# The front of a decoder's first stage put into one block

## The reference, cut to what matters

```python
xn1 = layernorm(x)                                   # outer norm, no weights
mu, var = mean(xn1), var(xn1)
xn = (xn1 - mu) * rsqrt(var + 1e-5) * norm_w + norm_b
xc, z = split(xn @ W_in)                             # 256 -> 2 x 512
xc = silu(conv4(xc) + conv_b)                        # causal, 4 taps
dbc = xc @ x_proj_w                                  # 512 -> 1 + 16 + 16
dt = softplus(dbc[:, :1] * dt_w + dt_b)
B, C = dbc[:, 1:17], dbc[:, 17:]
h = exp(dt * A) * h + dt * B * xc                    # over the tokens, 16 states
y = (h . C + xc * D) * silu(z)
x = x + (y @ W_out + xn1)
```

## Time and profile before

| | us |
|---|---|
| median of 3 runs | 2512.63 |
| lowest and highest | 2509.29, 2513.92 |
| the profiled execution | 2509.35 |
| its span, first to last instruction | 2507.6 |

### The profile page before, as it was taken

The page is one execution under the profiler, slowest core; times in us unless marked ns, Lnnn a source line. Parts: engine busy times, 40 slices in busy tenths (PEclk is TensorE's granted clock), DMA queues, the critical chain, the costliest instruction groups (busy, mean ns, idle before and its releaser), DMA issues. The chain is left out here.

```text
span 2507.6 us, 37343 instructions
## 1 busy us (share of the span) xinstructions
PE 1985.6 (79%) x10490; PEld 1106.8 (44%) x10490; DVE 1682.1 (67%) x3093; ACT 989.2 (39%) x2104; POOL 826.8 (33%) x603
## 2 busy tenths in 40 slices
PE   5945555557799898776999999978887799974777
PEld 2412222223466666333333333355444455542777
DVE  5769999993777777485555555556432466667994
ACT  2654333330577776225565555511211111111321
POOL 1036666560422220001666666610000022211342
PEclk8979999998899999897999999989989799986888
DMA  1024444441766663200455545353011421126220
GB/s 62 1 91 146 146 133 150 143 133 48 147 135 138 140 140 90 94 30 18 145 164 174 170 142 165 91 184 96 0 32 27 128 93 59 68 90 220 86 81 30
DMA packets 137566, 264.96 MB, mean 106 GB/s; under 512 B 34630, under 2 KB 89831, under 8 KB 134936
## 3 DMA queue, kind: packets, MB, share of 16 engines
q1 hardware_dynamic: 119864, 220.96, 30.0%
q0 software_dynamic: 13824, 37.77, 4.8%
q10 hardware_dynamic: 3808, 5.38, 0.8%
HBM read 214.61 MB, written 49.44 MB: 105 GB/s over the span
## 5 line engine op out<-in xcount | busy, mean ns | idle before, releaser
L552 PE MATMUL mamba_y<-mamba_read,ident 128*128 128x448 f32 x512 | 228.8, 571 | 162.6 <-DVE mamba_read L524 162.6
L500 POOL TENSOR_TENSOR xn<-mamba_u,mamba_b_all 128x896 f32<-128x896 f32 x128 | 263.3, 2078 | 259.7 <-DMA mamba_b_all<-mamba_b 259.7
L517 DVE TENSOR_TENSOR_SCAN mamba_state<-mamba_state,xn 128x896 f32<-128x896 f32 x128 | 258.9, 2023 | 6.5 <-POOL xn L500 6.0
L2378 ACT ACTIVATE moe_w_tile<-moe_w 128x1216 f32 x144 | 175.1, 1217 | 146.1 <-PE moe_y_ps L2330 131.8
L552 PEld LDWEIGHTS mamba_y<-mamba_read,ident 128*128 128x128 f32 x512 | 87.8, 191 | 303.2 <-DVE mamba_read L524 254.2
L2315 PE MATMUL moe_up_ps<-moe_w_tile,moe_xT 128*64 128x352 f32 x1152 | 204.3, 476 | 1.3 <-issue 1.3
L2277 POOL DMA_INDIRECT moe_y<-moe_y_sb,moe_index x144 | 158.0, 1097 | 108.5 <-DVE moe_y_sb L2351 75.6
L963 DVE CUSTOM_DVE_ANT_0 xattn_sm<-xattn_s_ps,xattn_mask 112x375 f32<-112x375 f32 x256 | 138.7, 545 | 80.9 <-PE xattn_s_ps L856 71.3
L1054 ACT ACTIVATE xattn_prob<-xattn_sm,xattn_least 112x375 f32<-112x375 f32 x256 | 154.4, 604 | 74.7 <-DVE xattn_least L963 70.8
L2330 PE MATMUL moe_y_ps<-moe_w_tile,moe_hT 128*64 128x256 f32 (+1 forms) x1152 | 177.3, 403 | 0.0
L2271 POOL DMA_INDIRECT moe_xg<-moe_tok,moe_index x144 | 152.8, 1061 | 53.6 <-issue 37.5
(11 more groups left out here) (310 smaller groups left out, 3931.4 us busy)
## 6 DMA issues: line engine op xcount, KB each, us to landing
moe_w<-moe_w SPq DMA_DIRECT2D x64, 480.0 KB
mamba_b_all<-mamba_b SPq DMA_DIRECT2D x64, 448.0 KB, 3.5
mamba_c_all<-mamba_c SPq DMA_DIRECT2D x64, 448.0 KB, 4.7
soft_w<-soft_w SPq DMA_DIRECT2D x16, 1024.0 KB, 8.4
moe_f_part<-moe_y SPq DMA_DIRECT2D x14, 1024.0 KB, 5.7
soft_logits<-soft_logit SPq DMA_DIRECT2D x28, 512.0 KB, 2.6
soft_logit<-soft_logits SPq DMA_DIRECT2D x14, 1024.0 KB, 5.2
xattn_ks<-xattn_k_parts SPq DMA_DIRECT2D x32, 375.0 KB, 6.5
```

What stands on the lines that cost most here:

```text
L500: pool.tensor_tensor(fed[:, PAIR * s + c], u[:, c0 + c, tok], b_all[:, s], ALU.mult).then_inc(input_ready, 1)
L517: dve.tensor_tensor_scan(state[:, q % 2, 0:HW], state[:, q % 2, 0:HW], fed[:, q % RING], 0.0, ALU.mult, ALU.add).then_inc(state_ready, 1)
L552: mm = pe.matmul(y[:, q % PAIR, w, 0:CW], g.ident[:], read[:, q % 2, w * CW:(w + 1) * CW], start=False, stop=False, skip_group_check=True)
L2378: pipelined(act, SLOT_TILES, RING, [weight_placer(act, 0, lambda to, src: act.activation(to, src, ACT.Copy)), silu, copy_hidden])
```

## The change

All work of the first stage up to the scan stands in one block.

- x is loaded in four chunks, each with a semaphore of its own that is kept across the stages, and the first block no longer waits for x or the identity. The stage's weights are issued at the start of the new block, and `dt_rep` is not loaded any more.
- The mean and the variance v of x are computed once. The outer norm is (x - m) / sqrt(v + e), and the second norm of it (x - m) / sqrt(v (1 + e) + e * e) before its weights; ACT takes both roots of the same variance. DVE makes the product with the second, ACT applies weight and bias. The first's reciprocal `r1` is taken by DVE, spread by PE in four one-row matmuls, copied by ACT, and POOL multiplies and adds it to x chunk by chunk.
- dt's column is the 33rd of the same product as B and C; its row is copied to SBUF with them and spread over the partitions by a one-row matmul (`spread_raw`).
- In softplus ACT copies `raw` to SBUF, and POOL does the linear part and the relu as eight tensor_scalar of 448 columns a chunk, and the sum. Exp and Ln are taken from one table set that has both.
- DVE's order is convolve 0, 1, then feed 0, convolve 2, feed 1, convolve 3, feed 2, feed 3, where `feed(j)` is the product with `xs`. A's exponential moves from the start of the block to its end. The first half of B and C is stored as soon as it is there.

```diff
-            sp.dma_start(g.x[:], ins["xT"].rearrange("(h p) t -> p h t", p=P)).then_inc(loaded, 16)
-            sp.dma_start(g.ident[:], ins["ident"]).then_inc(loaded, 16)
-            sp.wait_ge(loaded, 32)
+            x_in = ins["xT"].rearrange("(h p) t -> p h t", p=P)
+            for j in range(NCH):
+                sp.dma_start(g.x[:, :, chunk(j, CW)], x_in[:, :, chunk(j, CW)]).then_inc(g.x_loaded[j], 16)
+            sp.dma_start(g.ident[:], ins["ident"]).then_inc(g.ident_loaded, 16)
...
-            norm(g, g.x, xn1, prefetch=prefetch)
-            norm(g, xn1, g.xn, norm_wb[:, 0], norm_wb[:, 1], beside=add_residual)
...
+                @block.gpsimd
+                def _(pool):
+                    def residual(i):
+                        pool.wait_ge(r1_copied, i + 1)
+                        for h in range(DH):
+                            pool.tensor_tensor(xm[:, i, h], xm[:, i, h], r1[:, i], ALU.mult).then_inc(res_scaled, 1)
+                        pool.wait_ge(res_scaled, DH * (i + 1))
+                        x = g.x[:, :, chunk(i, CW)]
+                        pool.tensor_tensor(x, x, xm[:, i], ALU.add).then_inc(res_done, 1)
+                    def soften(j):
+                        pool.wait_ge(raw_copied, j + 1)
+                        for c in range(DIC):
+                            pool.tensor_scalar(u[:, c, chunk(j, CW)], raw_sb[:, j % 2], dt_w[:, c:c + 1], dt_b[:, c:c + 1], ALU.mult, ALU.add).then_inc(lin_done, 1)
+                        for c in range(DIC):
+                            pool.wait_ge(lin_done, DIC * j + c + 1)
+                            pool.tensor_scalar(u[:, c, chunk(j, CW)], u[:, c, chunk(j, CW)], 0.0, None, ALU.max).then_inc(relu_done, 1)
+                        for c in range(DIC):
+                            pool.wait_ge(ln_done, DIC * j + c + 1)
+                            pool.wait_ge(relu_done, DIC * j + c + 1)
+                            pool.tensor_tensor(dt[:, c, chunk(j, CW)], dt[:, c, chunk(j, CW)], u[:, c, chunk(j, CW)], ALU.add).then_inc(dt_done, 1)
+                    pool.wait_ge(normed, NCH)
+                    for i in range(NCH):
+                        residual(i)
+                    for j in range(NCH):
+                        soften(j)
...
-                            mm = pe.matmul(raw[:, 0:CW], dt_rep[:, c], xs[:, c, chunk(j, CW)], start=(c == 0), stop=(c == DIC - 1))
...
+                    def spread_raw(j):
+                        pe.wait_ge(bc_copied, j + 1)
+                        wait(pe, raw_copied, j)
+                        wait(pe, abs_done, DIC * j)
+                        pe.matmul(raw[:, 0:CW], g.ones[RAW:RAW + 1], bc_sb[RAW:RAW + 1, chunk(j, CW)], start=True, stop=True, tile_position=(RAW, 0)).then_inc(raw_ready, 1)
...
+                    pe.wait_ge(std1_ready, 1)
+                    project_xc(0)
+                    pe.wait_ge(normed, NCH)
+                    pe.wait_ge(rstd1_ready, len(parts))
+                    spread_r1(0)
+                    spread_r1(1)
+                    project_z(0)
+                    spread_r1(2)
+                    spread_r1(3)
+                    pe.wait_ge(small_loaded, 48)
+                    pe.wait_ge(r1_copied, NCH)
+                    for j in range(1, NCH):
+                        project_xc(j)
+                        derive(j - 1)
+                        project_z(j)
+                        spread_raw(j - 1)
+                    derive(NCH - 1)
+                    spread_raw(NCH - 1)
...
+                    convolve(0)
+                    convolve(1)
+                    for j in range(2, NCH):
+                        feed(j - 2)
+                        convolve(j)
+                    feed(NCH - 2)
+                    feed(NCH - 1)
...
+                        act.activation(raw_sb[:, j % 2], raw[:, 0:CW], ACT.Copy).then_inc(raw_copied, 1)
                         for c in range(DIC):
-                            act.activation(soft[:, c], raw[:, 0:CW], ACT.Abs, bias=dt_b[:, c:c + 1], scale=dt_w[:, c:c + 1]).then_inc(abs_done, 1)
-                            act.activation(relu[:, c], raw[:, 0:CW], ACT.Relu, bias=dt_b[:, c:c + 1], scale=dt_w[:, c:c + 1]).then_inc(raw_used, 1)
+                            act.activation(dt[:, c, chunk(j, CW)], raw[:, 0:CW], ACT.Abs, bias=dt_b[:, c:c + 1], scale=dt_w[:, c:c + 1]).then_inc(abs_done, 1)
+                        act.preload_act_table_set("natural_log_exp_and_others")
...
+                    act.activation(std[:], var[:, 0:CW], ACT.Sqrt, bias=g.eps2[:], scale=1.0 + EPS).then_inc(std_ready, 1)
+                    act.activation(std1[:], var[:, 0:CW], ACT.Sqrt, bias=g.eps[:]).then_inc(std1_ready, 1)
+                    act.wait_ge(small_loaded, 48)
+                    for i in range(NCH):
+                        affine(i)
+                    copy_r1(0)
+                    copy_r1(1)
+                    gates(0, 0, DIC)
+                    copy_r1(2)
+                    copy_r1(3)
+                    silus(0)
+                    for j in range(1, NCH):
+                        copy_bc(j - 1)
+                        gates(j, 0, DIC)
+                        silus(j)
+                        soften(j - 1)
+                    copy_bc(NCH - 1)
+                    soften(NCH - 1)
+                    act.activation(a_neg, a_neg, ACT.Exp).then_inc(a_exp, 1)
```

More of the change, by code:

```diff
@@ new lines, in _ @@
+                    for w, part in enumerate(parts):
+                        pe.wait_ge(rstd_ready, w + 1)
+                        for i in range(NCH):
+                            at = slice(i * ROWS, i * ROWS + 1)
+                            mm = pe.matmul(mean[:, i, part], g.ones[at], std[at, part], start=True, stop=True, tile_position=(i * ROWS, 0))
+                            if w == len(parts) - 1:
+                                mm.then_inc(spread, 1)
+                    pe.wait_ge(w_in_loaded, 16)
@@ L379, in convolve, with feed @@
                                     tap.then_inc(conv_done, 1)
[L381 to L387 removed]
+                    def feed(j):
                         for c in range(DIC):
```

182 lines of the change are left out of this document (112 added, 70 removed).

## The result

| | before, us | after, us |
|---|---|---|
| median (lowest, highest) of 7 runs each | 2512.63 (2508.12, 2516.82) | 2504.39 (2503.24, 2508.12) |
| profiled execution, its span | 2509.35, 2507.6 | 2508.12, 2506.3 |
| first mean starts | 8.29 | 4.32 |
| convolutions 0, 1, 2, 3 start | 57.80, 70.68, 88.17, 107.46 | 28.31, 44.88, 76.72, 103.44 |
| projection block ends | 150.9 | 143.98 |

The ratio of the times is 0.9972, 95% interval 0.996 to 0.9984, so 7 us less. The block's end moved by 6.9 us, the first scan step by 6.7 and the end of the scan's last VectorE product by 6.3: the scan did move along, but the block gave less than half of the forecast 15.6.

The account below looks back on a forecast made before the run. Waits between engines, not one busy engine, were taken to set the block's length; its end was to move from 150.9 to 135.3, 15.6 us earlier, giving 2497.0 on the median of 2512.63, range 2486 to 2509.

Parts of the forecast that it names:

- Part 4: Chunk products ahead of convolutions 2 and 3 wait for softplus; convolution 2 at 72.8, 12.3 us of the front's gain lost.
- Part 3: Convolution 0 to 1: projections, spreads and Silus take 14.8 us instead of 12.9, leaving a lead of 27.7 us.
- Part 1 and 2: Front: x in chunks starts the first mean at about 4.0; one statistic for both norms puts convolution 0 29.6 us earlier.
- rival B: GpSimd's tensor_scalar costs as two inputs, 1.0 us each; 5.7 us more, so 2503; chance 0.13.
- rival C: GpSimd's tensor_scalar is priced far from the copy; at 1.3 us each the whole lead is gone, then slower; chance 0.10.
- Rival A: VectorE and GpSimd do not hold each other up at sums and products; 5.9 us less, so 2491; chance 0.22.
- E: The product costs little since ScalarE gets through sooner; the lead of 27.7 at convolution 1 stays, 2485; chance 0.06.
- rival D: Exp and Ln still load separately, or x arrives later than read; 5.2 us more, 2502; chance 0.07.
- Convolution 2 to 3: Convolution, softplus steps, sums and products take 25.7 us instead of 19.3; convolution 3 at 98.5, lead 9.0.
- the end: From convolution 3 to the block's end 36.8 us instead of 43.4; end at 135.3 against 150.9.
- Table loads: Softplus drops its second load, leaving one of 1.3 us; the scan's 8 may go from ScalarE's idle time, for nothing.

Follow-up runs that it names:

- e12: Changed kernel with GpSimd's Relu replaced by multiply by 0 and add 0 (output wrong); block ends 93.8 us behind convolution 1, for 99.1.
- e13: e12 plus six idle TensorE matmuls and the wait for the r1 copies moved behind xc(1); block ends at 133.65 us.
- e1: Changed kernel with VectorE doing convolution j before the product of chunk j-2; ratio 0.989, block ends at 123.8 us.
- e4: Changed kernel plus eight one-input GpSimd operations of different forms, timed one at a time in chunk 1; 0.56 to 1.87 us each.
- e3: Changed kernel with the four sums of a chunk moved from GpSimd to VectorE; ratio 0.9918, block ends at 131.9 us.
- e2: Changed kernel with the four Relus of a chunk moved from GpSimd to VectorE; ratio 0.9922, block ends at 137.7 us.
- e8: Changed kernel with convolution j before the product of chunk j-2, and Relu and sum as one VectorE operation; ratio 0.9853, block ends at 115.3 us.
- e5: Changed kernel plus six TensorE matmuls whose results nobody reads, after the variances and the first rstd spreads; block ends at 139.1 us.
- e10: e8 plus six idle TensorE matmuls and the later wait for the r1 copies; ratio 0.9832, block ends at 110.1 us.

## Why the prediction was wrong

The forecast was 2497.0 and a block end of 135.3; measured were 2504.4 and 143.98. Direction and range held, the size didn't: of 15.6 us 6.9 came. Two terms of the sum were sized wrongly: in Part 4 the 0.57 us for each of GpSimd's eight operations, measured 0.70 and 1.30 (5.3 us, e12), and in Part 3 the 7.5 and 6.0 us for the projections xc(0) and xc(1), measured 8.68 and 7.95 (3.3 us beyond what the forecast had allowed, e13).

**Part 1 and 2** held. First mean at 4.32 (forecast 4.0), xc(0) at 24.18 (23.8), convolution 0 at 28.31 (28.2): its lead is 29.5 us, as forecast. That the two agree within 0.1 us is partly luck, since convolution 0 moves by 1.8 us between kernels with the same front. The residual on GpSimd cost nothing, and it was done at 51.94, before 62.35.

**Part 3** failed in one term, the length of a projection. xc(0) was taken over at 7.5 us from a row that was itself part slow; in the new place all of its beginning lies at the lower clock, 8.68. xc(1) was put at 6.0 and took 7.95, so that it ends 5.2 us behind the start of convolution 1 for the forecast 4.1; that is the 1.0 us by which Ln of chunk 0 is late behind convolution 1 (24.6 for 23.6). The spreads were cheaper than sized, 0.51 each for 0.75. I had let ScalarE's Silus set convolution 1, at 43.0; they ended at 43.8, and it was TensorE that came last, at 44.88.

**Part 4**: the mechanism was right, and it is what cost most (e1: 21.2 us of block). Wrong was the price of GpSimd's eight operations. The bounds were 0.57 and 1.0 each; the linear form has 0.70 and the Relu 1.30, so 1.0 on average and 8.0 us for the eight. That is rival B's number, with its 5.7 us against the 5.3 that e12 gives, and B's 2503 is 1.4 from the time. But B priced every one of the eight as an operation with two inputs, and neither form costs 1.0: that their average does is luck. By B the block would end at 141.0; most of the other 3.0 is Part 3's (1.8 up to convolution 1, 1.0 behind it). The nearest row was the copy, but a copy says nothing of a form of operation, and the spread between forms is a factor of three (e4). Sums and products together took 6.4 us in chunks 0 and 1, for the forecast 6.2: right sum, but they don't alternate there. The product stands until GpSimd's whole run of sums is over. In the last chunk they alternate as forecast, in 6.2 us. The Trainium skill (SBUF — State Buffer, "Who interferes with whom") has a VectorE instruction with two SBUF inputs contend with a GpSimd instruction that reads SBUF. The trace agrees (3.72 and 1.54 for 0.61 us), and in chunks 0 to 2 the hold-up lasted over a run of queued instructions. Two slips of the forecast changed little: a GpSimd row of the kernel before (L1758, 5.27 us at 2048 columns) lies at 2.6 ns a column, over the 2.3 that rival C takes as the most, and the chances of the forecast, A, E and D are 0.77 alone, so that "faster" with most of B is more than the 0.80 given.

**Convolution 2 to 3** is 1.0 longer, all of it the Relu (in e12 the products of chunks 0 and 1 are 25.7 us apart, 71.49 to 97.21, for the 26.7 of after), and **the end** 3.7 longer: in the last chunk all GpSimd's work is on the path. Its eight operations took 9.6 us (128.13 to 137.76) for the forecast 5.2. The Relus are 2.9 us over the price taken. The linear forms took 4.46 us for the forecast 2.8, two of them 1.5 each beside VectorE's products of chunk 2, which the forecast had sized as one delay of 0.5. Some 0.7 came back around the sums.

**Table loads.** Exp and Ln do share a load (64.72, then both), Exp begins 1.30 behind the start of the load as the forecast's Ln did, and the scan's eight are gone without effect: rival D is out. Rival A (no hold-up) is out by the products of 3.72 and 1.54 us, and by e3. Rival C, a price far from the copy, holds for half of the eight operations: the Relus have its 1.3, though with one constant and not with two per-partition operands.

## What to carry to other kernels

Before an engine is given a step that waits for a long chain, look what is queued behind it in the same engine: two lines exchanged gave 21 us of the block, where the whole change had given 7. Price an operation on GpSimd by a row of the same form; where none stands, keep the copy as the lower bound only. Where a projection is moved ahead, behind an idle TensorE, take its length at the lower clock, and see whether a few useless matmuls in the gap cost less than the lower clock does.

## What was not expected of the hardware

- GpSimd's one-input form at 128x448 fp32: multiply and add 0.56 us (constants) and 0.72 (per-partition scalars); one operation alone 1.33; pairs with a maximum 1.70 to 1.87. VectorE does the same Relu in 0.39 to 0.45 us (e2), but one beside a GpSimd sum took 1.32, and GpSimd's linear forms beside these Relus take 0.94 to 0.95 for 0.71. Maximum and add of two tensors in one VectorE operation take 0.62 (e8).
- A VectorE product with both inputs in SBUF, released by the first of four queued GpSimd sums, ended only after the fourth in chunks 0 to 2 (3.72 us for 0.61), while the sums kept their 1.12 to 1.13 us each. In the last chunk, and in chunks 0 to 2 of e12, the two took turns at about 1.5 us each. The eight took 6.2 to 6.5 us either way; on VectorE alone they take 4.4 (e3).
- The granted clock of 20 to 28 us is 0.50 where TensorE was idle for 2.3 and 2.8 us between small groups of matmuls, and 1.00 in e5, e10 and e13, where idle matmuls stand in these gaps; the next projection behind it is 2.4 us shorter.
